# Layer 1 of a convolution and state-space kernel: GpSimd in pairs of states, tap loads issued later, and the softplus put together on ScalarE and GpSimd

## What is computed

```python
x = silu(conv5x5_depthwise(x) + conv_b)          # 32 images, 96 channels, 3136 pixels
xs = x.reshape(B, C, L)
dts, Bs, Cs = split(einsum('kd,bdl->bkl', x_proj_w, xs))      # 6, 4 and 4 rows
delta = softplus(einsum('dr,brl->bdl', dt_w, dts) + dt_b)     # the step size
P = exp(cumsum(maximum(delta * A, log(1e-9)), axis=-1))       # for each of 4 states n
hs = P * cumsum(delta * Bs * xs / maximum(P, 1e-9), axis=-1)
y = sum over n of hs * Cs, + xs * Ds
```

## Time and profile before

| | us |
|---|---|
| median of 3 runs (4022.84 to 4023.77) | 4023.35 |
| the profiled execution's own time | 4020.36 |
| span of its trace | 4018.6 |
| first `gate` of layer 1 | 1957.93 |
| last `gate` of layer 1 | 4010.34 |

### The profile page before, as it was taken

The page is one execution under the profiler, slowest core; times in us unless marked ns, Lnnn a source line. Parts: engine busy times, 40 slices in busy tenths (PEclk is TensorE's granted clock), DMA queues, the critical chain, the costliest instruction groups (busy, mean ns, idle before and its releaser), DMA issues. The chain is left out here.

```text
span 4018.6 us, 72697 instructions
## 1 busy us (share of the span) xinstructions
PE 3650.8 (91%) x22358; PEld 2646.6 (66%) x22358; DVE 3106.0 (77%) x4416; ACT 2571.1 (64%) x4292; POOL 2575.8 (64%) x2672
## 2 busy tenths in 40 slices
PE   6999999999999999997899998998989989899776
PEld 6888787979787887877565564664646646466322
DVE  3675758475756667570499998999989989989999
ACT  1463728172735546274688787787778878777754
POOL 0352717162634536270488888888979889888988
PEclk9999999999999999998799898998989989989877
DMA  7546473747465554428565564655546646465222
GB/s 225 170 138 204 104 250 95 251 102 234 109 200 149 164 181 125 149 76 181 130 177 143 162 170 124 172 152 147 164 127 181 169 125 173 129 168 158 86 75 60
DMA packets 383746, 612.84 MB, mean 153 GB/s; under 512 B 199967, under 2 KB 324152, under 8 KB 383048
## 3 DMA queue, kind: packets, MB, share of 16 engines
q1 hardware_dynamic: 383336, 607.74, 53.5%
HBM read 527.35 MB, written 80.28 MB: 151 GB/s over the span
## 5 line engine op out<-in xcount | busy, mean ns | idle before, releaser
L321 POOL TENSOR_TENSOR h_low<-act_h,h_high 128x448 fp32r<-128x448 f32 x448 | 598.0, 1354 | 724.1 <-ACT h_high L520 723.9
L515 ACT ACTIVATE act_h<-ps_up,b 128x448 f32<-128x448 f32 x672 | 408.7, 635 | 728.5 <-PE ps_up L633 728.2
L1348 PE MATMUL ps_y<-h,ident 128*128 128x448 f32 x1344 | 727.1, 629 | 144.3 <-POOL h L1036 113.1
L1036 POOL TENSOR_TENSOR h<-h,c_rows 128x448 f32<-128x448 f32 x672 | 763.7, 1136 | 51.2 <-DVE h L1126 5.7
L1023 POOL TENSOR_TENSOR u<-dxs,b_rows 128x448 f32<-128x448 f32 x672 | 764.5, 1138 | 27.9 <-DVE ps_q L1115 16.8
L1099 DVE TENSOR_TENSOR_SCAN ps_q<-d_a,q_last,ps_q 128x448 f32<-128x448 f32 x576 | 659.5, 1145 | 0.0
L1126 DVE TENSOR_TENSOR_SCAN h<-d_a,h_last,ps_q 128x448 f32<-128x448 f32 x576 | 645.3, 1120 | 0.0
L1300 PEld LDWEIGHTS ps_front<-win,taps 120*112 120x112 f32 x4608 | 540.5, 188 | 149.2 <-issue 147.2
L606 PE MATMUL ps_stage<-win,taps 124*112 124x112 f32 x6144 | 608.3, 261 | 2.7 <-DVE w_low L368 2.7
L606 PEld LDWEIGHTS ps_stage<-win,taps 124*112 124x112 f32 x6144 | 608.1, 178 | 3.2 <-DVE w_low L368 2.8
L1205 ACT ACTIVATE d_a<-delta,log_eps,a_neg 128x448 f32<-128x448 f32 x672 | 503.3, 750 | 114.0 <-DVE h L1126 58.5
(11 more groups left out here) (81 smaller groups left out, 6212.6 us busy)
## 6 DMA issues: line engine op xcount, KB each, us to landing
taps<-in_t_dram SPq DMA_DIRECT2D x192, 896.0 KB, 5.0
taps<-in_t_dram SPq DMA_DIRECT2D x192, 672.0 KB, 4.7
b_rows<-bc_dram SPq DMA_DIRECT2D x224, 224.0 KB, 3.0
c_rows<-bc_dram SPq DMA_DIRECT2D x224, 224.0 KB, 3.1
xres<-in_x_dram SPq DMA_DIRECT2D x224, 168.0 KB, 2.5
x_dram<-x1o SPq DMA_DIRECT2D x224, 168.0 KB, 2.0
x1pad<-x_dram SPq DMA_DIRECT2D x96, 392.0 KB, 6.0
out_dram<-y SPq DMA_DIRECT2D x168, 224.0 KB, 2.6
```

The costliest lines, as they stand in the source:

```text
L321: nc.gpsimd.tensor_tensor(h_low[u % 2][:, t, :], act_h[u % 2][:, t, :], h_high[u % 2][:, t, :], ALU.subtract).then_inc(h_low_ready[t], 1)
L515: nc.scalar.activation(act_h[u % 2][:, t, :], ps_up[t][:, 0:BT], ACT.Gelu, bias=b1[:, t:t + 1]).then_inc(gelu_done, 1)
L1036: nc.gpsimd.tensor_tensor(h[s % H_SLOTS][:, :], h[s % H_SLOTS][:, :], c_rows[n][:, :], ALU.mult).then_inc(hc_done, 1)
L1348: nc.tensor.matmul(total, ident[:, :], h[s % H_SLOTS][:, :], start=False, stop=(n == N - 1)).then_inc(y_added, 1)
```

## The change

GpSimd's `times_b` and `times_c` now treat two states in one instruction (`b_rows`, `c_rows`, `u` and `h` become tiles with a second axis); one iteration of its loop is a pair p of steps, with `times_b` of pair p + 1 ahead of `times_c` of pair p - 1. `u` has 2 pairs, `h` 3 pairs (6 steps as before). `sum_delta` leaves VectorE: ScalarE writes max(z, 0) as a `Relu` into `delta` between `Abs` and `Exp` (so `ZSTEPS` is 4), and GpSimd adds the logarithm in place. `delta_rows` and `project` on TensorE wait for the `Relu` and no longer for the sum. On SP, the loads for the front work come last in a step, and not before the step at which their buffer should be free.

```diff
-ZSTEPS = 3
-U_SLOTS = 3
-U_AHEAD = U_SLOTS
-H_SLOTS = 6
+ZSTEPS = 4
+U_PAIRS = 2
+U_SLOTS = 2 * U_PAIRS
+H_PAIRS = 3
+H_SLOTS = 2 * H_PAIRS
...
-        SUM_AT = (7, 9, 11)
-        DXS_AT, DXS_NOW = (8, 10), 1
+        SUM_AT, SUM_NOW = {3: 0, 4: 1}, {0: 2}
+        DXS_AT, DXS_NOW = {4: 0, 5: 1}, {1: 2}
...
+            def begin_at(load, k, unit):
+                last_use = {load_slab: turn_unit, load_taps: conv_unit}[load]
+                slots, pieces = {load_slab: (SLABS, 1), load_taps: (SLOTS2, HALVES)}[load]
+                free = unit_step[last_use[k - slots]] + pieces + 1 if k >= slots else 0
+                return max(unit_step[unit] - AHEAD, free)
...
-                todo = loads[SLABS:] if ahead else []
+                todo = sorted(loads[SLABS:], key=lambda load: begin_at(*load)) if ahead else []
                 for s in range(S):
...
-                    while todo and unit_step[todo[0][2]] <= s + AHEAD:
-                        load, k, _ = todo.pop(0)
-                        load(g + 1, False, k)
                     if ahead or b + 1 < BANDS:
                         if j == STORE_XD_AT:
                             store_xd(f, fb)
...
                         store(g, (s - N - Y_LAG - 1) // N)
+                    while todo and begin_at(*todo[0]) <= s:
+                        load, k, _ = todo.pop(0)
+                        load(g + 1, False, k)
...
+            def sum_delta(f, b, t):
+                n = f * RUNS + b * TILES + t + 1
+                pool.wait_ge(z_step, n * ZSTEPS)
+                nc.gpsimd.tensor_tensor(delta[:, t, :], delta[:, t, :], z_log[t % Z_SLOTS][:, :],
+                                        ALU.add).then_inc(delta_ready, 1)
...
+            def times_b(g, p, first=False):
...
-                    pool.wait_ge(gated, g * S + s - U_SLOTS + 2)
-                nc.gpsimd.tensor_tensor(u[s % U_SLOTS][:, :], dxs[:, t, :], b_rows[n][:, :],
-                                        ALU.mult).then_inc(u_done, 1)
+                    pool.wait_ge(gated, g * S + 2 * p + 1 - U_SLOTS + 2)
+                nc.gpsimd.tensor_tensor(u[p % U_PAIRS][:, :, :], dxs[:, t, :].unsqueeze(1).broadcast_to([128, 2, BT]),
+                                        b_rows[:, n:n + 2, :], ALU.mult).then_inc(u_done, 2)
...
+            def times_c(g, p):
...
+                pool.wait_ge(h_done, g * S + 2 * p + 3)
                 if b + 1 < BANDS:
...
+                    nc.gpsimd.tensor_tensor(h_last[:, j:j + 2], pair[:, :, BT - 1], zeros[:, 0:2],
+                                            ALU.add).then_inc(h_kept, 2)
+                    pool.wait_ge(h_kept, g * KEPT + 2 * p + 2)
+                nc.gpsimd.tensor_tensor(pair[:, :, :], pair[:, :, :], c_rows[:, n:n + 2, :],
+                                        ALU.mult).then_inc(hc_done, 2)
...
+                for p in range(S // 2):
+                    b, j = 2 * p // STEPS, 2 * p % STEPS // 2
...
+                    if prepare and 2 * (j + 1) == STEPS - N:
+
+                        pool.wait_ge(xd_stored, (f * BANDS + fb + 1) * 16)
+                    if p + 1 < S // 2:
+                        times_b(g, p + 1, p == 0 and first)
+                    elif more:
+                        times_b(g + 1, 0)
+                    if p > 0:
+                        times_c(g, p - 1)
+                    if prepare and j in SUM_AT:
+                        sum_delta(f, fb, SUM_AT[j])
+                    if j in SUM_NOW:
+                        sum_delta(g, b, SUM_NOW[j])
                     if prepare and j in DXS_AT:
...
-            def sum_delta(f, b, t, first=False):
...
-                nc.vector.scalar_tensor_tensor(delta[:, t, :], z_bank(t)[:, 0:BT], 0.0, z_log[t % Z_SLOTS][:, :],
-                                               ALU.max, ALU.add).then_inc(delta_ready, 1)
...
                 nc.scalar.activation(z, z_bank(t)[:, 0:BT], ACT.Abs).then_inc(z_step, 1)
+                if not first:
+
+                    act.wait_ge(clipped, (f * BANDS + b - 1) * STEPS + (t + 1) * N)
+                    act.wait_ge(dxs_ready, f * RUNS + (b - 1) * TILES + t + 1)
+                nc.scalar.activation(delta[:, t, :], z_bank(t)[:, 0:BT], ACT.Relu).then_inc(z_step, 1)
                 act.wait_ge(z_step, n + 1)
                 nc.scalar.activation(z, z, ACT.Exp, scale=-1.0).then_inc(z_step, 1)
```

More of the change, by code:

```diff
@@ L751, in layer1 @@
         d_a = [sb(f"d_a{i}", [128, BT]) for i in range(DA_SLOTS)]
-        b_rows = [sb(f"b_rows{i}", [128, BT]) for i in range(N)]
-        u = [sb(f"u{i}", [128, BT]) for i in range(U_SLOTS)]
-        c_rows = [sb(f"c_rows{i}", [128, BT]) for i in range(N)]
-        h = [sb(f"h{i}", [128, BT]) for i in range(H_SLOTS)]
+        b_rows = sb("b_rows", [128, N, BT])
+        u = [sb(f"u{i}", [128, 2, BT]) for i in range(U_PAIRS)]
+        c_rows = sb("c_rows", [128, N, BT])
+        h = [sb(f"h{i}", [128, 2, BT]) for i in range(H_PAIRS)]
         q_last = sb("q_last", [128, STEPS])
@@ L1012, in times_x @@
                                         ALU.mult).then_inc(dxs_ready, 1)
-            def times_b(g, s, first=False):
-                b, t, n = s // STEPS, s % STEPS // N, s % N
+            def times_b(g, p, first=False):
+                t, n = 2 * p % STEPS // N, 2 * p % N
                 if t == 0:
-                    pool.wait_ge(b_in[n], (g * BANDS + b + 1) * 16)
+                    for k in (n, n + 1):
+                        pool.wait_ge(b_in[k], (g * BANDS + 2 * p // STEPS + 1) * 16)
@@ L1029, in times_c @@
+                nc.gpsimd.tensor_tensor(u[p % U_PAIRS][:, :, :], dxs[:, t, :].unsqueeze(1).broadcast_to([128, 2, BT]),
+                                        b_rows[:, n:n + 2, :], ALU.mult).then_inc(u_done, 2)
+            def times_c(g, p):
+                b, j, t, n = 2 * p // STEPS, 2 * p % STEPS, 2 * p % STEPS // N, 2 * p % N
+                pair = h[p % H_PAIRS]
                 if t == 0:
[L1030 to L1031 removed]
+                    for k in (n, n + 1):
+                        pool.wait_ge(c_in[k], (g * BANDS + b + 1) * 16)
+                pool.wait_ge(h_done, g * S + 2 * p + 3)
@@ L1043, in group @@
                     prepare = more or b + 1 < BANDS
-                    if s > 0:
-                        times_c(g, s - 1)
-                    if prepare and j in DXS_AT:
-                        times_x(f, fb, DXS_AT.index(j))
-                    if j == DXS_NOW:
-                        times_x(g, b, TILES - 1, b == 0 and first)
-                    if prepare and j + U_AHEAD == STEPS - N:
-                        pool.wait_ge(xd_stored, (f * BANDS + fb + 1) * 16)
-                    if s + U_AHEAD < S:
-                        times_b(g, s + U_AHEAD)
-                    elif more:
-                        times_b(g + 1, s + U_AHEAD - S)
@@ L1061, in _ @@
+                    if j in SUM_NOW:
+                        sum_delta(g, b, SUM_NOW[j])
+                    if prepare and j in DXS_AT:
+                        times_x(f, fb, DXS_AT[j])
+                    if j in DXS_NOW:
+                        times_x(g, b, DXS_NOW[j], b == 0 and first)
+                times_c(g, S // 2 - 1)
             for t in range(TILES - 1):
+                sum_delta(0, 0, t)
                 times_x(0, 0, t, True)
-            for s in range(U_AHEAD):
-                times_b(0, s, True)
+            times_b(0, 0, True)
@@ L1135, in group @@
                     gate(g, s)
-                    if (more or b + 1 < BANDS) and j in SUM_AT:
-                        sum_delta(f, fb, SUM_AT.index(j))
                     if s + 1 < S:
@@ L1140, in group @@
                     scan_h(g, s)
-            for t in range(TILES):
-                sum_delta(0, 0, t, True)
             if last:
```

37 lines of the change are left out of this document (10 added, 27 removed).

## The result

The changed kernel takes **4054.68 us** (median of 4 runs, 4046.61 to 4058.57) against 4023.1 us of four runs of the kernel before on the same chip: ratio **1.0071**, 95% interval 1.0050 to 1.0092. It is slower by some 29 us where 95 us less were forecast, and lies outside the range. The profiled execution took 4057.06 us, its span is 4055.2.

A forecast was written before the change was run, and what follows sets the result against it. Layer 1 was taken as bound by VectorE's instruction stream, plus disturbances at group starts and in the last two bands. 4020.4 - 87.5 - 75.7 + 29 + 28 + 7 + 4 = 3925.2, so 3928 us as median; range 3880 to 3980.

The forecast's parts named there:

- The sum leaves VectorE, 87.5 us: On VectorE: 165 sums of 0.53 us come off, counted in full wherever VectorE sets the pace.
- Pairs at 2.04 us: On GpSimd: one 896-column pair instruction costs 2.04 us, from the price per column, against 2.18 for two single ones.
- GpSimd's 1.0 us of slack: On GpSimd: 32.6 us of work a band against VectorE's 33.6, leaving 1.0 us where it had 2.5.
- The waits for the logarithm leave VectorE, and `u` may be 5 us late: VectorE's 39.6 us of waits move to GpSimd's queue; some 5 us of lateness exceeds the longest wait, 3.8 us.
- Slower: Rival: GpSimd's queue, waiting for the logarithm, delays h, TensorE and the next logarithm; 4115 us, chance 0.03.
- the ring: Late `sum_delta` on GpSimd delays h, TensorE's step, the next projection and the next logarithm; 4115 us, chance 0.03.
- 2.6 us of waits a band: Threshold on GpSimd, 35.2 - 32.6 us a band, above which its waits would make the ring decide.
- Relu, 7 us: On ScalarE: the added Relu, 0.53 us each, matters at 6 of 21 places; 1.0 us a group, seven groups.
- Tap and window loads later, 36.1 us: On SP's queue: C rows no longer stuck behind these loads; most of VectorE's 36.1 us of waits for `u` go.
- What comes back, 57 us: VectorE waits returning in seven groups: 29 us after step 72 and 28 us at the groups' starts.
- The lock: Rival: longer GpSimd instructions hold the port shared with VectorE 0.95 us longer; about 4575 us, chance 0.01.

The follow-up runs named there:

- e2: Changed kernel with the sums back on VectorE and no Relu; pairs and new load order kept: 4053.53 us, 1.0065 to the kernel before.
- e14: Kernel before with new load order and pairs for `u` only; products of h single, sums on VectorE: 3991.01 us, ratio 0.9924, timed again 0.9931.
- e5: Changed kernel whose GpSimd additions wait only for the Relu, not the logarithm (step size added to itself): 3989.1 us, 0.9892 to the kernel before.
- e3: Kernel before with the new load order alone, single states: 4015.64 us, ratio 0.9976.
- e10: Kernel before with the new load order and one extra, overwritten Relu on ScalarE per tile and band: 4057.0 us, ratio 1.0058.
- e15: Kernel before with new load order and only the third tile's sum on GpSimd, timed in more rounds: 3997.66 us, ratio 0.9938.
- e16: Kernel before with the new load order alone, timed again in more rounds: 4015.9 us, ratio 0.9979.
- e12: Kernel before, single states, with new load order, all three sums on GpSimd and the Relu on ScalarE: 4031.6 us, ratio 1.0020.
- e9: Changed kernel with neither the addition nor the wait for the logarithm on GpSimd: 3987.53 us, 0.9902 to the kernel before.
- e13: Changed kernel without ScalarE's Relu; GpSimd adds the logarithm to itself after the same wait: 4017.92 us, 0.9984 to the kernel before.
- e7: Changed kernel with the first tile's sum back on VectorE, without its Relu; other two on GpSimd: 4047.73 us, 1.0034 to the kernel before.

## Why the prediction was wrong

- *The sum leaves VectorE, 87.5 us.* Right. 165 sums went. In the last group, without front work, 18 sums make 9.5 us, and 8.4 came: 1.6 us, all of it, in each band that has sums, but 0.5 in band 0.
- *Pairs at 2.04 us.* Right as a price. **What failed is that only the `u` of a pair was asked how late it may be; the product of h was given no price.** It waits for two scans and, with GpSimd's queue not full, comes after 5.4 and 2.6 us (e2) where a single one came after 1.7; TensorE's sum with it ends 2.8 us later than with single products. Priced at 0, measured at 55 us (e2 against e14), of which 46.9 are VectorE's wait for the logarithm.
- *GpSimd's 1.0 us of slack.* It was 0.1: 0.34 us from `h_last` to `h` where the earlier trace rows have 0.27 for one column, and 0.3 for a `u` behind its own `dxs`, which the kernel before hid in its longer lead.
- *The waits for the logarithm leave VectorE, and `u` may be 5 us late.* This is the second failed step. The 5 us were set against the longest single wait, but in a queue without slack the waits add up: 39.6 us on VectorE became 100.4 us on GpSimd, and VectorE then waited 99.7 us for `u` in 85 pieces. Taking the wait out brings that to 11.3 and gives 72 us (e5). The rival *Slower* named this wait, with a chance of 0.03, but it works otherwise than told there: through `u`, while the late product of `h` and the ring behind it stayed in e5 as the time fell. The point from which that rival decides was set at 2.6 us of waits a band; the 100.4 us are less than 2 a band and were enough.
- *Relu, 7 us.* The third. Measured 33 us alone and 35 in the changed kernel. The step counted 0.5 us at six of 21 places and took a third of that. What the runs show in its place is a longer wait for the logarithm (69.5 to 109.0 us) and a lower granted clock of TensorE (e3 against e10), neither of which the step considered. How half a microsecond of ScalarE comes to cost so much is open.
- *Tap and window loads later, 36.1 us.* Oversized. Alone it gave 0.2%, 9 us: the waits for `u` went, but the wait for the logarithm rose from 39.6 to 69.5 us, as if an earlier VectorE only met the lateness of the logarithm sooner. In the changed kernel it is worth 70 us.
- *What comes back, 57 us.* Of the right kind, too small: 206.1 us of VectorE's waits stand against the 67 that the sum had left (85.7 - 75.7 + 57). These 139 us are the miss (4057.1 - 3925.2 = 132). By place, in the middle groups: 8.9 us a group in band 0 where 4 were taken, 11.4 in bands 5 and 6 where 4.1 were, and 10.9 in bands 1 to 4, to which the sum gave nothing.
- *The lock* did not occur: beside pairs of 2.09 us VectorE's steps stay at 2.80. The trace agrees there with what the Trainium skill (SBUF — State Buffer, "Who interferes with whom") leaves free, an instruction with one of its inputs in PSUM. Its GPSIMD Engine Reference ("Engine selection") advises against two-input elementwise work on GpSimd; of three sums a band one moved gains 0.4% (e15 against e16), three in single states lose as much (e12 against e3), so here the advice was nearer than the sum that set it aside.

The parts don't add: Relu (35), late products (55) and the wait (72) make 162 us, more than the 132 us of the miss. Each was priced by itself, and no run here prices them together. **Open** is why the decays stay so late in e5, e9 and e13 (95 to 108 us of VectorE's waits in each), though each took one suspect away. The runs show this much: with all sums on VectorE (e2) that wait is 3.1 us, but VectorE waits 101.3 us for the logarithm; with the first tile's sum alone back on VectorE (e7) it is 8.1 and 158.8. It looks as if ScalarE were late in each case and VectorE met it at whichever of the two it needs first. What makes ScalarE late is not shown; TensorE's low clock at the group's start is a candidate that no run tests. A version with single products of h and all three sums on GpSimd, which would have 35.5 us of GpSimd's work, was not tried.

## What to carry to other kernels

When an engine's work is regrouped into longer instructions, price not only the work saved but the moment at which the first half of the result is there, and follow it through every in-order queue behind it. A wait moved from the engine that sets the pace to a helper's queue is free only as far as that queue's slack in each band, counted with every start gap, and a full queue turns small disturbances into lost time (the old load order cost 9 us on the old queue and 70 on the full one). When a wait is gone from the list, ask where the same engine will be waited for next. And read the granted clock beside each ratio before a difference is put down to the edit's own few instructions. Where three such moves are possible, try one.

## What had not been expected of the hardware

- A GpSimd instruction that waits for a one-column or two-column one just before it on its own queue starts 0.34 us after that one started with two columns (median of the changed kernel's; 2856.59 to 2856.91 is 0.32), 0.27 with one (median in e14; 2876.55 to 2876.81 is 0.26). A `u` of 896 columns behind a `dxs` that it needs starts 1.44 us after it, where independent ones start 1.10 apart.
- The kernel before varies from chip to chip and run to run between 4010.6 and 4053.7 us, and its mean granted clock with it: 0.933 in the former execution, 0.919 in the latter. Undisturbed steps of VectorE are 2.80 us in both kernels. Within one execution the clock of band 0 is 0.80 in one group and 0.62 in another, and the band lasts 40.4 and 43.8 us (groups 3 and 5 of the kernel before).
